# Row statistics for the second layer, taken in a round of attention instead of among the expert units

## The chip, the cores and the metric

The kernel runs on one core of one Trainium2 chip. The metric is the device time of one execution in microseconds (us); lower is better. Five engines of the core work side by side, each through its own queue in program order: TensorE (PE in the profile, with its weight loads as PEld), VectorE (DVE), ScalarE (ACT), GpSimd (POOL) and SyncE (SP), which issues the DMAs. They wait for each other through semaphores. "Busy" shares of different engines overlap.

## The reference, cut to what matters

Two layers work on x of shape (8 batches, 512 rows, 128 columns). In outline:

```
xn = layernorm(x)                                  # per row
x  = x + attention0(xn) + experts(xn)              # 16 heads of 64, causal; 32 experts, top 6, and a shared one
xn = layernorm(x)                                  # per row: mean and variance of the NEW x
x  = x + attention1(xn) + ffn1(xn)                 # attention1 starts with an RMS norm of xn
```

The change concerns the second `layernorm`: for each row of the new x, the mean m and the variance v, then 1/sqrt(v + eps), and beside it the root that the RMS norm of the normalized row needs, 1/sqrt(v/(v + eps) + eps_rms).

## The kernel before

The first layer handles one batch after the other, b = 0 to 7. A batch has two phases.

**Rounds.** Attention of the first layer goes in 8 rounds (`PAIRS`), p = 0 to 7, with two heads in a round. TensorE computes the scores of round p in three chunks (`score0`, the last one, chunk 2, only when the exponentials of chunk 0 are done, L1526), ScalarE takes the exponentials (L731), TensorE turns (transposes) the blocks of probabilities of round p - 1 in five steps (`turn_step`, L1391), VectorE copies four of the turned banks out of PSUM (`take_turned`, L1074) and ScalarE the fifth, and TensorE multiplies them with the values (`weigh_pair`, L1413). So the slot of round p on TensorE holds the turns and the weighing of round p - 1. VectorE also takes the maxima of each row of scores (`row_maxima`, L1083), before which no exponential of the chunk can start.

The order of the steps on each engine is written out by hand. On VectorE a round p > 0 is: copy turned steps 0 and 1 of the round before; maxima of chunk 0; `invert_sums`; `rest_q` (in round 7 `add_rows` instead, which adds the first layer's result of the batch before to x); copy steps 3 and 2; maxima of chunk 2; `rest_k` (not in round 7); maxima of chunk 1; and at the end `route(b, p)`, one piece per round of the choice of experts. In rounds 6 and 7 that piece is the first-layer statistics of the next batch: `stats0` (four `bn_stats`, L972) and `variances0` (L978, L980); for the last batch there is neither.

Two waits tie TensorE to this order. Turn step 4 writes the PSUM bank that step 0 used, so it waits for VectorE's copy of step 0 (`pe.wait_ge(pt_ready, rnd * (TURNS - 1) + 1)`). And chunk 2 of the scores waits for the exponentials of chunk 0, which wait for their maxima.

**Units.** Then 17 expert units, u = 0 to 16 (`units`): TensorE projects a unit (L64 to L66), ScalarE takes a SiLU, VectorE multiplies (`gate` L1112, `hidden` L1122), the result is split in a high and a low part (ScalarE, and VectorE L1116 or GpSimd L541), and TensorE multiplies with the down weights. Between the units stands the preparation of the next batch: rows are normalized after unit 1, and from unit 12 on the next batch's values are projected.

**Statistics for the second layer.** `row_stats(b, ...)` issues on VectorE four `bn_stats` (L1181), a wait for them, four `bn_aggr` (L1184), a wait for them, and two small `tensor_scalar` (L1186, L1187); the last raises `x1_var_ready`. `inv_sqrt1(b)` issues on GpSimd six small operations (L589 to L594), the first and the last of them powers of -0.5; it raises `x1_rstd_ready`. Before the change, batch b - 1's `row_stats` stands in unit 12 of batch b (b = 1 to 6), and its `inv_sqrt1` follows after all of GpSimd's unit work of batch b. The new rows of batch b - 1 are complete in round 7 of batch b (`add_rows`). The first reader of any of these results is `norm_rows1`, in unit 5 of batch 7. Batches 6 and 7 have their statistics taken inside the second layer, which the change leaves alone.

GpSimd has nothing to do in the rounds but `inv_sqrt0(b + 1)` (L508), which waits for `variances0` of round 7; after it come its low parts and divisions of the units.

Of the kernel before, what the change touches and what calls it, by code (L numbers as in the profile page):

```python
# [15 lines left out]
B, T, D = 8, 512, 128  # L16
# [65 lines left out]
def build(nc, a, out_dram):  # L82
    with ExitStack() as ctx:
        def sb(name, shape, dt=F32):
            return ctx.enter_context(nc.sbuf_tensor(name, shape, dt))

        def sem(name):
            return ctx.enter_context(nc.semaphore(name))


        x_all = sb("x_all", [P, B, TILES, D])
# [241 lines left out]
        x1_var_ready = sem("x1_var_ready")  # L333
# [53 lines left out]

        NORM_AFTER, STATS1_AFTER, ROWS_AFTER, LOGITS_AFTER, QK_AFTER, V_AFTER = 1, 12, 5, 7, 9, 12  # L390

        ROWS1_AFTER, TURN1_AFTER = [5, 7, 9], [8, 10, 12]

# [103 lines left out]
        def _(pool):  # L497
# [7 lines left out]
            def inv_sqrt0(b):  # L505
                s = slice(b * TILES, (b + 1) * TILES)
                pool.wait_ge(var_ready, b + 1)
                pool.tensor_tensor(rstd[:, s], var[:, s], mhalf[:, s], ALU.pow).then_inc(rstd_ready, 1)  # L508
# [34 lines left out]
            def units(b):  # L543
                for u in POOL_LO:
                    low_part(b, u)
                    for p in POOL_LO[u]:
                        divide_pair(b, p)

            def split_down(k):
                u = DOWN_PIECES[k]  # L550
                pool.wait_ge(down_hi_ready, k + 1)
                pool.tensor_tensor(down_lo[:, u, :], down_raw[:, u, :], down_hi[:, u, :].bitcast(F32), ALU.subtract).then_inc(down_lo_ready, 1)
# [23 lines left out]
            def second_layer_weights():  # L576
                for part in range(3):
                    bias_part(part)
                setup.step(pool.tensor_copy(wf, qw))
                setup.step(pool.tensor_scalar(wf, wf, 1.0 / 7.5, -1.0, ALU.mult, ALU.add))  # L580
                setup.step(pool.tensor_tensor(wf, wf, qs, ALU.mult))
                pool.wait_ge(lora_taken, 2)
                pool.tensor_tensor(lin[:, :, :], lin[:, :, :], wf, ALU.add).then_inc(lin_ready, 1)

            def inv_sqrt1(b):

                s = slice(b * TILES, (b + 1) * TILES)
                pool.wait_ge(x1_var_ready, b + 1)
                setup.step(pool.tensor_tensor(rstd[:, s], var[:, s], mhalf[:, s], ALU.pow))  # L589
                pool.tensor_tensor(nmr[:, s], nmean[:, s], rstd[:, s], ALU.mult)  # L590
                setup.step(pool.tensor_tensor(rsmall[:, 1, s], rstd[:, s], rstd[:, s], ALU.mult))
                setup.step(pool.tensor_tensor(rsmall[:, 1, s], rsmall[:, 1, s], mv[:, s, 1], ALU.mult))
                setup.step(pool.tensor_scalar(rsmall[:, 1, s], rsmall[:, 1, s], EPS_RMS, None, ALU.add))
                pool.tensor_tensor(rsmall[:, 0, s], rsmall[:, 1, s], mhalf[:, s], ALU.pow).then_inc(x1_rstd_ready, 1)  # L594
# [4 lines left out]
            for k in range(len(DOWN_PIECES)):  # L599
                split_down(k)  # L600
            for b in range(B):
                if b < B - 1:
                    inv_sqrt0(b + 1)
                units(b)
                if b == 0:
                    second_layer_weights()
                elif b < B - 1:
                    inv_sqrt1(b - 1)
            for q in range(GROUPS):
                n0 = q * G  # L610

# [354 lines left out]
        def _(dve):  # L966
# [47 lines left out]
            def route_probabilities(b):  # L1014
                dve.wait_ge(rexp_done, b + 1)
                chain.step(dve.tensor_reduce(sm, rexp[:, :, :], AX, ALU.add))
                chain.step(dve.reciprocal(ri, sm))
                chain.step(dve.tensor_tensor(rl[:, :, :], rexp[:, :, :], over_experts(ri), ALU.mult))
                chain.step(dve.tensor_tensor(chosen, rl[:, :, :], ebias[:, :].unsqueeze(1).to_broadcast([P, TILES, E]), ALU.add))

            def route_top():
                for t in range(TILES):
                    last = dve.max(top8[:, t, :], corr[:, t, 0:E])
                chain.step(last)
                chain.step(dve.memset(top8[:, :, TOPK:8], GONE))

            def route_mark():
                dve.wait_ge(mask_ready, 1)
                for t in range(TILES):
                    last = dve.match_replace(left[:, t, :], top8[:, t, :], corr[:, t, :], TAKEN)  # L1030
                chain.step(last)
# [9 lines left out]
            def route_divide():  # L1041
                chain.step(dve.reciprocal(ri, sm))
                dve.tensor_tensor(comb_et, comb[:, :, :], over_experts(ri), ALU.mult).then_inc(comb_ready, 1)

            def route(b, p):
                if p == 1:
                    route_probabilities(b)
                if p == 2:
                    route_top()
                if p == 3:  # L1050
                    route_mark()
                if p == 4:
                    route_weights(b)
                if p == 5:
                    route_divide()
                if p == 6 and b < B - 1:
                    stats0(b + 1)
                if p == 7 and b < B - 1:
                    variances0(b + 1)
# [69 lines left out]
            def first_layer(b):  # L1129
                for p in range(PAIRS):  # L1130
                    n = b * PAIRS + p
                    if p == 0:
                        row_maxima(n, 0)
                        row_maxima(n, 1)
                        rest_q(n + 1, SCALE0)
                        rest_k(n + 1)
                        row_maxima(n, 2)
                    else:
                        take_turned(n - 1, range(0, 2))
                        row_maxima(n, 0)  # L1140
                        invert_sums(n - 1)
                        if p < PAIRS - 1:
                            rest_q(n + 1, SCALE0)
                        elif b:
                            add_rows(b - 1)
                        take_turned(n - 1, [3, 2])
                        row_maxima(n, 2)
                        if p < PAIRS - 1:
                            rest_k(n + 1)
                        row_maxima(n, 1)  # L1150
                    route(b, p)
                n = b * PAIRS + PAIRS - 1
                take_turned(n, range(0, 2))
                invert_sums(n)
                for u in range(UNITS):
                    if u == 0:
                        take_turned(n, [3, 2])
                    gate(b * UNITS + u, u)
                    if u:
                        hidden(b, u)  # L1160
                    if u and u - 1 not in POOL_LO:
                        low_part(b * UNITS + u - 1, u - 1)
                    if b < B - 1:
                        if u == NORM_AFTER:
                            norm_rows(b + 1, xn)
                    if 0 < b < B - 1 and u == STATS1_AFTER:
                        row_stats(b - 1, x_all[:, b - 1, :, :], x1_var_ready)
                    if b < B - 1:
                        if u == ROWS_AFTER:
                            split_xt(b + 1)  # L1170
                        if u == LOGITS_AFTER:
                            take_logits(b + 1)
                        if u == QK_AFTER:
                            rest_q((b + 1) * PAIRS, SCALE0)
                            rest_k((b + 1) * PAIRS)
                low_part(b * UNITS + UNITS - 1, UNITS - 1)

            def row_stats(b, src, out_sem):
                s = slice(b * TILES, (b + 1) * TILES)
                for t in range(TILES):  # L1180
                    last = dve.bn_stats(stats[:, b * TILES + t, :], src[:, t, :])  # L1181
                chain.step(last)
                for t in range(TILES):
                    last = dve.bn_aggr(mv[:, b * TILES + t, :], stats[:, b * TILES + t, :])  # L1184
                chain.step(last)
                dve.tensor_scalar(nmean[:, s], mv[:, s, 0], -1.0, None, ALU.mult)  # L1186
                dve.tensor_scalar(var[:, s], mv[:, s, 1], EPS, None, ALU.add).then_inc(out_sem, 1)  # L1187
# [8 lines left out]
            for b in range(B):  # L1196
                first_layer(b)
# [9 lines left out]
            for q in range(GROUPS):  # L1207
# [57 lines left out]
                for r in range(2 * G + 1):  # L1265
# [19 lines left out]
                    if q == 0 and r in (3, 5):  # L1285
                        b = B - 2 + r // 4
# [576 lines left out]
```

## Time and profile before

| | |
|---|---|
| median of 3 runs | 1237.54 us (1235.39 to 1241.89) |
| the profiled execution, its own time | 1236.49 us |
| span of the profile, first to last instruction | 1234.7 us |
| PE / DVE / ACT / POOL busy | 97% / 79% / 67% / 33% |
| granted TensorE clock, mean | 0.996 of full speed |

A timeline row gives the start, the duration, the engine, the line, the operation, output<-inputs by the program's names, shapes, and how many in a row were merged ("x2"); in brackets stands the idle time of the engine just before it and what ended it. Names of tiles that share memory are sometimes taken for one another (a hidden activation can be called qk_lo, the third buffer of the gates probs). Ends of matmuls are modelled, so their starts are what can be compared. Times are us from the span's start.

### The profile page before, as it was taken

The page shows a single profiled execution, that of the slowest core. Times are in us where ns is not written, and L with a number is a line of the kernel's source. Part 1 is how long each engine was busy: PE and PEld are TensorE (multiplying, and loading weights), DVE is VectorE, ACT ScalarE, POOL GpSimd, SP SyncE. Part 2 cuts the span into 40 slices and gives each one's busy share as a digit, 9 for nine tenths or more (in the row PEclk, how much of TensorE's full clock was granted, in tenths as well). Part 3 has the DMA queues.
Part 4 walks back from the last instruction along what each step waited for, and adds up shares of the span by engine and source line. Part 5 has one row for each costly group of instructions (what it writes and reads, how often), then busy time and mean ns, then how long its engine had stood idle before and what let it go on. Part 6 is the DMA issues. An engine that isn't in the chain of part 4 may idle for free.

```text
span 1234.7 us, 25147 instructions
## 1 busy us (share of the span) xinstructions
PE 1199.8 (97%) x9508; PEld 903.2 (73%) x9508; DVE 981.3 (79%) x1898; ACT 822.4 (67%) x2173; POOL 412.3 (33%) x371
## 2 busy tenths in 40 slices
PE   6999999999999999999999999999999999998997
PEld 4777777767776777777867786778677767767775
DVE  5888588868896889688968896889687876888785
ACT  6775577557756775677557755775576667676775
POOL 1336420640063006300730072007200859326910
PEclk9999999999999999999999999999999999999999
DMA  7004300410041004100410040015001500000000
GB/s 252 2 19 138 98 1 20 130 60 2 27 128 55 2 29 135 46 2 29 146 36 1 29 150 31 2 30 162 17 2 39 171 1 1 10 11 18 2 10 27
DMA packets 44280, 64.01 MB, mean 52 GB/s; under 512 B 8128, under 2 KB 18368, under 8 KB 43904
## 3 DMA queue, kind: packets, MB, share of 16 engines
q1 hardware_dynamic: 44160, 62.39, 16.0%
q8 instruction: 77, 1.26, 0.4%
q14 instruction: 43, 0.35, 0.1%
HBM read 59.48 MB, written 2.88 MB: 51 GB/s over the span
## 4 chain that ended last, share of the span: by engine, by line
PE 83%; DVE 7%; ACT 4%; POOL 3%; DMA 1%; issue 1%; SPq 1%; POOLq 0%; DVEq 0%
PE psum L1391 14%; PE psum L1363 14%; PE psum L1413 12%; PE psum L64 10%; PE psum L66 10%; PE psum L65 10%; PE psum L1452 4%; PE psum L1368 2%; ACT probs L731 2%; PE psum L1322 1%; PE psum L1417 1%; DVE mneg L1083 1%; DVE stats L1181 1%; PE psum L1618 1%; DMA crow<-weights 1%
## 5 line engine op out<-in xcount | busy, mean ns | idle before, releaser
L731 ACT ACTIVATE probs<-psum,mneg 128x512 f32<-128x512 f32 (+3 forms) x640 | 330.4, 530 | 142.5 <-DVE mneg L1083 138.2
L1083 DVE TENSOR_REDUCE mneg<-psum 128x2 f32<-128x1024 f32 (+2 forms) x320 | 254.2, 820 | 124.6 <-PE psum L1368 121.8
L1391 PE MATMUL psum<-ident,probs 128*128 128x128 f32 x1600 | 225.9, 279 | 9.0 <-ACT pt L752 3.7
L1074 DVE COPY pt<-psum 128x512 f32<-128x512 f32 x320 | 206.1, 683 | 30.0 <-PE psum L1391 27.6
L1391 PEld LDWEIGHTS psum<-ident,probs 128*128 128x128 f32 x1600 | 177.5, 141 | 42.9 <-issue 24.0
L541 POOL TENSOR_TENSOR qk_lo<-sg,qk_hi 128x512 fp32r<-128x512 f32 x64 | 91.9, 1442 | 167.4 <-ACT qk_hi L775 167.4
L508 POOL TENSOR_TENSOR rstd<-var,mhalf 128x4 f32<-128x4 f32 x8 | 8.1, 1018 | 409.4 <-DVE var L980 409.4
L1413 PE MATMUL psum<-pt,v_all 128*64 128x384 f32 (+5 forms) x1088 | 142.6, 412 | 0.0
L731 ACT ACTIVATION_READ_ACCUMULATOR probs<-psum,mneg 128x1 f32 x640 | 131.9, 206 | 0.0
L1363 PE MATMUL psum<-qk_hi 64*128 64x512 f32 (+7 forms) x640 | 122.8, 379 | 1.2 <-ACT probs L731 1.1
L1413 PEld LDWEIGHTS psum<-pt,v_all 128*64 128x64 f32 (+1 forms) x1088 | 69.7, 135 | 63.0 <-issue 50.6
L64 PE MATMUL psum<-xt_hi,gu_hi 128*128 128x512 f32 x272 | 110.8, 408 | 0.4 <-DVE sg L1112 0.4
L65 PE MATMUL psum<-xt_lo,gu_hi 128*128 128x512 f32 x272 | 107.6, 396 | 0.0
L66 PE MATMUL psum<-xt_hi,gu_lo 128*128 128x512 f32 x272 | 107.2, 394 | 0.0
L537 POOL TENSOR_TENSOR yt<-yt,rrow 128x512 f32<-128x512 f32 x64 | 99.5, 1559 | 23.2 <-DMA rrow<-sums 22.9
L1122 DVE TENSOR_TENSOR sg<-sg,crow 128x512 f32<-128x512 f32 x88 | 97.6, 1109 | 7.3 <-DMA crow<-weights 4.4
L1363 PE MATMUL psum<-qk_lo,qk_hi 64*128 64x512 f32 (+7 forms) x640 | 103.2, 318 | 0.0
L1363 PE MATMUL psum<-qk_hi,qk_lo 64*128 64x512 f32 (+7 forms) x640 | 103.0, 317 | 0.0
L785 ACT ACTIVATE sg<-psum 128x512 f32<-128x512 f32 x96 | 57.2, 596 | 58.0 <-PE psum L66 57.9
L1363 PEld LDWEIGHTS psum<-qk_hi 64*128 64x128 f32 (+1 forms) x640 | 60.1, 184 | 45.9 <-issue 44.4
L1112 DVE TENSOR_TENSOR sg<-sg,psum 128x512 f32<-128x512 f32 x96 | 65.3, 680 | 23.3 <-ACT sg L785 23.3
L775 ACT ACTIVATE qk_hi<-sg 128x512 fp32r<-128x512 f32 x96 | 60.3, 628 | 29.1 <-DVE sg L1122 29.1
(255 smaller groups left out, 2460.7 us busy)
## 6 DMA issues: line engine op xcount, KB each, us to landing
crow<-weights SPq DMA_DIRECT2D x256, 128.0 KB, 2.9
rrow<-sums SPq DMA_DIRECT2D x128, 128.0 KB, 3.0
gu_raw<-in_gu SPq DMA_DIRECT2D x1, 2176.0 KB, 11.6
x_all<-in_x SPq DMA_DIRECT2D x8, 256.0 KB, 5.4
out_rows<-x_all SPq DMA_DIRECT2D x8, 256.0 KB, 2.3
down_raw<-in_down SPq DMA_DIRECT2D x1, 1088.0 KB, 13.7
wqkv_raw<-in_wqkv SPq DMA_DIRECT2D x1, 896.0 KB, 6.9
wqkv_raw<-in_wqkv SPq DMA_DIRECT2D x1, 512.0 KB, 5.1
```

Of the source, the lines that this page charges most:

```text
L64: nc.tensor.matmul(out, lh, rh, start=start, stop=False, **kw)
L65: nc.tensor.matmul(out, lh, rl, start=False, stop=False, **kw)
L66: return nc.tensor.matmul(out, ll, rh, start=False, stop=stop, **kw)
L537: pool.tensor_tensor(yt[:, p, :], yt[:, p, :], rrow[:, n % RROWS, :], ALU.mult).then_inc(y_divided, 1)
L541: pool.tensor_tensor(hm_lo[u % 3], sg[u % 3], hm_hi[u % 3].bitcast(F32), ALU.subtract).then_inc(pool_lo_ready, 1)
L731: last = act.activation(probs[:, h * HALF + PROB[t]:h * HALF + PROB[t] + w], bank[score_bank(rnd, c) + h][:, o:o + w], ACT.Exp, bias=mneg[ ...
L1074: dve.tensor_copy(turned_rows(rnd)[:, s % 2, :, 3 - s // 2, :], bank[TURN_BANK[s]].rearrange("p (j q) -> p j q", q=P)).then_inc(pt_ready, 1)
L1083: last = dve.tensor_reduce(mneg_h[:, :, t], psum[:, b:b + 2, o:o + P * (t + 1)], AX, ALU.max, negate=True)
L1122: dve.tensor_tensor(sg[u % 3], sg[u % 3], crow[:, m % CROWS, :], ALU.mult).then_inc(hm_ready, 1)
L1363: mm(bank[score_bank(rnd, c) + h][:, o:o + w], ql[r, 0, qs_], kl[r, 1, ks], start=i == 0 and n == 0, stop=False, **K)
L1391: last = nc.tensor.transpose(bank[TURN_BANK[s]][:, i * P:(i + 1) * P], probs[:, v:v + P], ident[:, :])
L1413: last = mm(Y[c:c + m, first * P:T], v(k), rows_t[:, k, first:TILES, :].rearrange("p t q -> p (t q)"), start=(k == 0), stop=(k == TILES - ...
```

## The change

`row_stats` leaves unit 12 of batch b (for batch b - 1) and is issued in round 6 of batch b, behind `route`, for batch b - 2 (b = 2 to 7). `inv_sqrt1` of that batch is issued on GpSimd ahead of `inv_sqrt0(b + 1)` and of the units of batch b, instead of behind the units. Both still cover batches 0 to 5.

```diff
-        NORM_AFTER, STATS1_AFTER, ROWS_AFTER, LOGITS_AFTER, QK_AFTER, V_AFTER = 1, 12, 5, 7, 9, 12
+        NORM_AFTER, ROWS_AFTER, LOGITS_AFTER, QK_AFTER, V_AFTER = 1, 5, 7, 9, 12
+
+        STATS1_ROUND = 6
@@ GpSimd
             for b in range(B):
+                if b > 1:
+                    inv_sqrt1(b - 2)
                 if b < B - 1:
                     inv_sqrt0(b + 1)
                 units(b)
                 if b == 0:
                     second_layer_weights()
-                elif b < B - 1:
-                    inv_sqrt1(b - 1)
@@ VectorE, rounds of first_layer
                     route(b, p)
+                    if b > 1 and p == STATS1_ROUND:
+                        row_stats(b - 2, x_all[:, b - 2, :, :], x1_var_ready)
@@ VectorE, units of first_layer
-                    if 0 < b < B - 1 and u == STATS1_AFTER:
-                        row_stats(b - 1, x_all[:, b - 1, :, :], x1_var_ready)
```

## Rows read from the trace of the kernel before

**Rows 1.** The page, part 1: busy us (share), instructions of each engine.
```profile
PE 1199.8 (97%) x9508; PEld 903.2 (73%) x9508; DVE 981.3 (79%) x1898; ACT 822.4 (67%) x2173; POOL 412.3 (33%) x371
```

**Rows 2.** Stretch, length, busy PE PEld DVE ACT POOL (instructions), clock, DMA, GB/s.
```profile
281.35:403.24 121.89, 121.89 (x905) 90.87 (x907) 100.24 (x177) 79.53 (x209) 33.37 (x26) 1.00 0.17 54
...
768.76:890.41 121.65, 121.65 (x907) 90.94 (x907) 99.82 (x177) 79.62 (x209) 33.44 (x26) 1.00 0.17 54
...
325.38:333.37 7.99, 7.99 (x87) 6.17 (x89) 7.54 (x15) 5.66 (x19) 0.00 (x0) 1.00 0.01 2
```

**Rows 3.** Waits of TensorE's weight loads, 150 to 955 us: us in total, times, longest.
```profile
PEld psum L64 <- DVE sg L1112: 2.7, 6, 0.8
...
PEld psum L64 <- ACT v_all L740: 1.1, 3, 0.4
```

**Rows 4.** Timeline of VectorE, batch 2, end of round 6 and round 7.
```profile
326.62 1.28 DVE L1083 TENSOR_REDUCE mneg<-psum 128x2 f32<-128x768 f32 x2
327.82 0.86 DVE L972 BATCH_NORM_STATS2 stats<-x_all 128x6 f32<-128x128 f32 x4
328.72 1.29 DVE L1074 COPY pt<-psum 128x512 f32<-128x512 f32 x2
329.92 1.22 DVE L1083 TENSOR_REDUCE mneg<-psum 128x2 f32<-128x1024 f32 x1
...
331.72 1.28 DVE L1074 COPY pt<-psum 128x512 f32<-128x512 f32 x2
333.41 1.56 DVE L1083 TENSOR_REDUCE mneg<-psum 128x2 f32<-128x512 f32 x2 [0.41 <-PE psum L1368]
```

**Rows 5.** Timeline of TensorE, slot 7 of batch 2.
```profile
329.61 0.66 PE L1391 MATMUL psum<-ident,probs 128*128 128x128 f32 x4
...
332.68 0.39 PE L1363 MATMUL psum<-qk_hi 64*128 64x256 f32 x2
...
333.30 2.16 PE L1413 MATMUL psum<-pt,v_all 128*64 128x384 f32 x16
```

**Rows 6.** Timeline of ScalarE, last step of chunk 0's exponentials, round 7 of batch 2.
```profile
332.43 0.20 ACT L731 ACTIVATION_READ_ACCUMULATOR probs<-psum,mneg 128x1 f32 x1
```

**Rows 7.** Timeline of VectorE, units 12 and after, batch 2.
```profile
373.16 0.86 DVE L1181 BATCH_NORM_STATS2 stats<-x_all 128x6 f32<-128x128 f32 x4
...
374.62 0.68 DVE L1112 TENSOR_TENSOR sg<-sg,psum 128x512 f32<-128x512 f32 x1
...
379.74 0.69 DVE L1112 TENSOR_TENSOR sg<-sg,psum 128x512 f32<-128x512 f32 x1 [1.06 <-ACT sg L785]
```

**Rows 8.** Timeline of TensorE, the late start at unit 12, batch 2.
```profile
366.75 0.51 PE L64 MATMUL psum<-xt_hi,gu_hi 128*128 128x512 f32 x1
```

**Rows 9.** Timeline of VectorE, batch 7, end of round 6 and round 7.
```profile
935.69 1.28 DVE L1083 TENSOR_REDUCE mneg<-psum 128x2 f32<-128x768 f32 x2
937.38 1.29 DVE L1074 COPY pt<-psum 128x512 f32<-128x512 f32 x2 [0.41 <-PE psum L1391]
938.79 1.23 DVE L1083 TENSOR_REDUCE mneg<-psum 128x2 f32<-128x1024 f32 x1
```

**Rows 10.** Timeline of TensorE, chunk 2 of the scores, round 7 of batch 7.
```profile
941.73 0.36 PE L1363 MATMUL psum<-qk_hi 64*128 64x256 f32 x2
```

**Rows 11.** Timeline of GpSimd, batch 2: the root in round 7, and inv_sqrt1's first and last.
```profile
335.87 1.01 POOL L508 TENSOR_TENSOR rstd<-var,mhalf 128x4 f32<-128x4 f32 x1 [70.25 <-DVE var L980]
...
382.27 1.45 POOL L589 TENSOR_TENSOR rstd<-var,mhalf 128x4 f32<-128x4 f32 x1
...
386.18 1.03 POOL L594 TENSOR_TENSOR rsmall<-rsmall,mhalf 128x4 f32<-128x4 f32 x1
```

**Rows 12.** Lines L1186, L980, L1094: duration ns min/median/max, first and last start us.
```profile
L1186 DVE TENSOR_SCALAR nmean<-mv x32: 169/170/1204, 252.3 to 1154.1; 128x4 f32<-128x4 f32 x32
L980 DVE TENSOR_SCALAR var<-mv x8: 169/170/171, 4.9 to 823.0; 128x4 f32<-128x4 f32 x8
L1094 DVE RECIPROCAL rinv<-rsum x80: 190/193/205, 31.0 to 1224.7; 128x8 f32<-128x8 f32 x80
```

## The prediction

> **What bounds the kernel now.** I read the page's busy shares first [rows 1]: TensorE 97%, VectorE 79%, ScalarE 67%, GpSimd 33%. That names a suspect, no more. Next the busy time by stretch [rows 2]: from the first weighing of one batch to that of the next (121.9 us in batch 2, 121.65 in batch 6) TensorE's busy time is equal to the length of the stretch, at the full granted clock, and VectorE is busy 100 of 122 us. Then the waits [rows 3]: over the first layer from 150 us on, TensorE's weight loads wait six times for `gate` (2.7 us in all) and three times for a copied value bank (1.1 us); nothing else of weight holds TensorE up. So the first layer is one dense queue of TensorE work. A microsecond that another engine saves gives nothing unless it removes one of those few waits, and a microsecond by which another engine comes late where TensorE has no reserve is added whole.
>
> What matters is therefore the reserve at the two places, old and new, and not VectorE's share.
>
> **The work moved, on VectorE.** In unit 12 of batch 2 the four `bn_stats` begin at 373.16 and the next `gate` at 374.62 [rows 7]: `row_stats` takes 1.46 us of VectorE's time, its two chain waits included. (One of its small operations, L1186, is 0.17 us in the median and 1.20 at most [rows 12], so in some batches it holds VectorE about a microsecond longer in the old place.)
>
> **What the removal gives.** The `gate` of 374.62 comes up to 1.46 us earlier in batches 1 to 6. VectorE catches up by itself: it stands idle 1.06 us before the gate at 379.74, waiting for ScalarE [rows 7]. The late start of TensorE in these units, at 366.75 [rows 8], comes more than six microseconds before the statistics begin at 373.16, so it isn't theirs. I found no late TensorE start between them and the end of the units. I take 0. The bounds: at best all of the waits in [rows 3] go, 2.7 + 1.1 = 3.8 us; at worst nothing.
>
> **What the addition costs, batches 2 to 6.** VectorE in round 6 of batch 2 [rows 4]: the last maxima start at 326.62, `stats0` at 327.82, the copies of turned steps 0 and 1 at 328.72, the maxima of chunk 0 of round 7 at 329.92. No idle time stands between these rows: VectorE arrives there behind TensorE's turns, with nothing to give. `row_stats` goes between 327.82's group and 328.72, and all that follows moves by 1.46 us. Two waits of TensorE hang on it:
> - Turn step 4 starts at 329.61 [rows 5] and needs the copy of step 0. Two copies take 1.29 us from 328.72 [rows 4], so the first ends near 329.37, and the reserve is about 0.24 us. TensorE would stand some 1.2 us here.
> - Chunk 2 of the scores starts at 332.68 [rows 5]. It needs the exponentials of chunk 0, whose last instruction ends at 332.43 + 0.20 = 332.63 [rows 6]: no reserve at all. These exponentials follow maxima that start at 329.92 and move by 1.46. The two delays run beside each other, since the 1.2 us of the first are part of the same lateness: the maxima need a bank that TensorE wrote before turn 4. So by chunk 2 TensorE is 1.46 us late in all.
> - The weighing at 333.30 [rows 5] needs copies that begin at 331.72 and end 1.28 us later, at 333.00 [rows 4]; both sides move by 1.46, so nothing is added.
>
> After that VectorE again waits for TensorE (0.41 us before 333.41 [rows 4]); its backlog is gone, but TensorE's is not, as its queue has no idle time later in which to make it up. The cost is 1.46 us a batch, for the five batches 2 to 6: 7.3 us.
>
> **Batch 7.** It has no `stats0`, so `row_stats` fills some of that room. Its last maxima start at 935.69 [rows 9]; in batch 2 the next group began 327.82 - 326.62 = 1.20 us after that [rows 4], here 936.89. Plus 1.46 gives copies at 938.35, and the maxima of chunk 0 1.21 us later, at 939.56, against 938.79 before [rows 9]. In batch 2 chunk 2 could start 332.68 - 329.92 = 2.76 us after the start of those maxima [rows 4, 5], here 942.32, against 941.73 [rows 10]: 0.6 us. The first layer loses 7.3 + 0.6 = 7.9 us.
>
> **The roots on GpSimd.** They ran behind the units and nobody waited; their removal there gives 0. In the new place they start when `row_stats` ends, near 328.72 + 1.46 = 330.2, and from first start to last end they took 386.18 + 1.03 - 382.27 = 4.94 us [rows 11]: done near 335.1. The root that the next batch waits for starts at 335.87 before and 1.46 later after [rows 11]. They fit in front of it, so it isn't late, and GpSimd has no work in slot 7 (0.00 busy) up to the next weighing [rows 2]. I take 0; the bounds are 0 and a root late by as much as the six operations last, 4.9 us.
>
> One more thing is to be weighed. VectorE's small `tensor_scalar` L1186 is 169 to 1204 ns, while the reciprocal L1094 stays within 190 to 205 over 80 times and L980, which has GpSimd idle beside it, at 169 to 171 [rows 12]. So a form like L1186 can be held up to 1.03 us by a running GpSimd instruction, and a reciprocal has not been. In the new slot the roots run beside VectorE's work of round 7.
> The Trainium skill ("SBUF — State Buffer", Who interferes with whom) has it that VectorE and GpSimd share a port pair that is locked for a whole instruction, and that `tensor_scalar` can take it. The spread of L1186 agrees. By that rule L980 would be the one at risk in the new place, which is the third rival below.
>
> **Second layer.** It starts from batch 7 and moves with it; the first reader of the roots in unit 5 of batch 7 asks for batch 0 to 2, whose roots are done batches before. 0. No DMA is issued or moved; SP's stores of the experts' weights start from TensorE's turn in slot 7 and move along with it.
>
> **The sum.** 1236.49 + 7.9 = 1244.4 on the profiled execution's own time. The median of the runs shown is 1237.54, 1.05 above that execution, and would give 1245.4. I take the middle, 1244.9. What this kernel's measurement can tell from no change is about 0.5%, 6.2 us, so slower begins at 1243.7.
>
> **Rivals.**
> 1. *Not slower: the lateness is absorbed.* Place: the copy of step 0 and the maxima of chunk 0. For it: VectorE has idle time in the slot, 7.99 - 7.54 = 0.45 us by the stretch [rows 2], more in others, and TensorE's ends are modelled, so a reserve may be hidden in its records. Against: 332.63 against 332.68, and L1363 at 332.68 waits in the code. If TensorE had a hidden reserve of 1.46 us in each of these six places, the rounds would cost 0, and the units would give 0 to 3.8 us: 1236.5 down to 1232.7 on the profiled execution, 1233.8 to 1237.5 by the median. It decides at a reserve of 1.46 us; below that the rest is paid. Half of the lateness hidden (0.73) gives about 1240.5.
> 2. *The two waits add up instead of running beside each other*: 1.22 + 1.46 us a batch, because ScalarE's copy of turn 4 stands ahead of the exponentials in its queue. 5 x 2.68 = 13.4, and some 1 us in batch 7: 1251 to 1252. Against: the moved copy by ScalarE would be ready before the moved maxima.
> 3. *GpSimd's roots hold VectorE's L980* by up to 1.03 us in five batches, of which some hides in the idle time behind it: at most 5 x 1.03 = 5.2 more, 1250; I would expect half of it, 1247.5. Against: the roots should be done near 335.1, before L980.
>
> **How the numbers follow.** Forecast 0.74, of it some 0.05 under 1243.7; absorbed wholly or by half 0.17 (wholly, with a gain over 0.5%, 0.03); added waits 0.04; contention 0.05. The forecast's own range is 1243 to 1248. For 8 in 10 the range is 1240.5 to 1249: it takes in half of the lateness absorbed and the likely contention. Faster by over 0.5%: 0.03. Slower: 0.69 + 0.04 + 0.05 = 0.78, less what the two medians can wander: 0.74. Same: 0.23.
>
> **What would show it.** In the changed kernel: copies in round 7 starting 1.4 to 1.5 us later behind `stats0`; an idle time of TensorE before turn step 4 of about 1.2 us released by L1074, and a short one before chunk 2 released by L731; the slot between two weighings 9.45 us in place of 7.99 in batches 2 to 6, 8.6 in batch 7, and unchanged in batch 1, which has no new work there; batches 2 to 6 each 1.46 us longer; the stretch of units as long as before. I am wrong if slot 7 keeps 7.99 (a reserve that I don't see), if the units shorten (a wait of unit 12 that I missed), or if the next batch's rows come late behind GpSimd.

## The result, and the profile after

The changed kernel takes 1248.45 us (median of 4 runs, 1247.31 to 1248.66) against 1237.34 us for the kernel before (4 runs, 1235.39 to 1241.89). The ratio is 1.008, 95% interval 1.006 to 1.010: slower by 7 to 12 us. The forecast was 1244.9 us in a range of 1240.5 to 1249.0. A later measurement of the same kernel, beside 23 runs of the one before, gave 1.0068 (1.0056 to 1.008), which is 8.4 us (6.9 to 9.9).

The page, part 1, of the kernel after, to be held against [rows 1]. All shares are as they were; a share doesn't show this change.
```profile
PE 1203.8 (97%) x9508; PEld 906.1 (73%) x9508; DVE 985.3 (79%) x1898; ACT 822.4 (66%) x2173; POOL 403.4 (32%) x371
```
The stretch shows it. The same slot 7 of batch 2, from the weighing of round 5 to that of round 6 (length, busy PE, PEld, DVE, ACT, POOL, clock): 9.45 us in place of 7.99 [rows 2]. (The row of before lies 0.07 us behind the weighings at both ends; by their starts they stand at 325.31 and 333.30, which gives the same 7.99.) TensorE's busy time is now less than its stretch, by 1.34 us; GpSimd has 2.82 us of roots there.
```profile
328.40:337.85 9.45, 8.11 (x90) 6.20 (x86) 8.94 (x25) 5.66 (x19) 2.82 (x6) 1.00 0.01 2
```
VectorE in that slot, kernel after, answers to [rows 4]. Its lines have moved by two.
```profile
329.71 1.28 DVE L1085 TENSOR_REDUCE mneg<-psum 128x2 f32<-128x768 f32 x2
330.91 0.86 DVE L974 BATCH_NORM_STATS2 stats<-x_all 128x6 f32<-128x128 f32 x4
331.81 0.87 DVE L1183 BATCH_NORM_STATS2 stats<-x_all 128x6 f32<-128x128 f32 x4
332.71 0.38 DVE L1186 BATCH_NORM_AGGREGATE mv<-stats 128x2 f32<-128x6 f32 x4
333.13 0.17 DVE L1188 TENSOR_SCALAR nmean<-mv 128x4 f32<-128x4 f32 x1
333.20 0.17 DVE L1189 TENSOR_SCALAR var<-mv 128x4 f32<-128x4 f32 x1
333.27 1.28 DVE L1076 COPY pt<-psum 128x512 f32<-128x512 f32 x2
334.47 1.22 DVE L1085 TENSOR_REDUCE mneg<-psum 128x2 f32<-128x1024 f32 x1
...
337.96 1.89 DVE L1085 TENSOR_REDUCE mneg<-psum 128x2 f32<-128x512 f32 x3 [0.41 <-PE psum L1370]
```
The copies follow `stats0`'s start by 333.27 - 330.91 = 2.36 us, before by 0.90: 1.46 more. The idle 0.41 us at the end is there as before: VectorE is level with TensorE again, and the lateness is now TensorE's.

TensorE in the same slot answers to [rows 5]: the scores of chunk 0 end, then a wait, turn step 4, chunk 2 (337.23), the weighing.
```profile
332.54 0.23 PE L1370 MATMUL psum<-hide,later 64*128 64x64 bf16 x4
334.11 0.63 PE L1393 MATMUL psum<-ident,probs 128*128 128x128 f32 x4 [1.34 <-DVE pt L1076]
...
337.23 0.39 PE L1365 MATMUL psum<-qk_hi 64*128 64x256 f32 x2
...
337.85 2.16 PE L1415 MATMUL psum<-pt,v_all 128*64 128x384 f32 x16
```
Counted from the weighing that begins the slot (325.31 before, 328.40 after), turn step 4 starts 1.41 us later than before and chunk 2 1.46 us later.

ScalarE's last step of the chunk 0 exponentials, as in [rows 6]: it ends at 337.18, and chunk 2 starts 0.05 us behind it.
```profile
336.98 0.20 ACT L733 ACTIVATION_READ_ACCUMULATOR probs<-psum,mneg 128x1 f32 x1
```
GpSimd's first and last instruction of `inv_sqrt1` and the root that follows, answering to [rows 11]. The six end at 336.60, and the root of the next batch starts 3.8 us later.
```profile
333.45 1.01 POOL L591 TENSOR_TENSOR rstd<-var,mhalf 128x4 f32<-128x4 f32 x1 [69.26 <-DVE var L1189]
...
335.56 1.04 POOL L596 TENSOR_TENSOR rsmall<-rsmall,mhalf 128x4 f32<-128x4 f32 x1
340.41 1.01 POOL L510 TENSOR_TENSOR rstd<-var,mhalf 128x4 f32<-128x4 f32 x1 [3.81 <-DVE var L982]
```
TensorE's waits for VectorE's copies over the first layer from 150 us on (total, times, longest). Before there was none; now there are six, one for each batch with the new work: 1.34 us in batches 2 to 6 and 0.43 in batch 7.
```profile
PE psum L1393 <- DVE pt L1076: 7.1, 6, 1.3
```

**Where the time went.** The spans differ by 1245.5 - 1234.7 = 10.8 us. I split them at the weighings. Slots behind round 6: 9.45, 9.46, 9.44, 9.45, 9.45 in batches 2 to 6 in place of 7.99 each, and 8.54 in place of 7.96 in batch 7: 7.30 + 0.58 = 7.88 us. The rest of the way from the first weighing to the last: 0.47 (in all 924.54 against 916.19). Behind the last weighing: some 0.35 less. Ahead of the first weighing: 2.82 us (36.40 against 33.58), before any instruction that the change touched.

Those 2.82 us are TensorE's rate at the start. Matmuls of 512 columns, kernel before, then kernel after, in the projection of the values: starts 0.24 us apart before, 0.43 us after, where the closer spacing began at 20.97.
```profile
16.57 0.39 PE L65 MATMUL psum<-wqkv_lo,xt_hi 128*128 128x512 f32 x1
16.81 0.40 PE L66 MATMUL psum<-wqkv_hi,xt_lo 128*128 128x512 f32 x1
```
```profile
18.41 0.63 PE L65 MATMUL psum<-wqkv_lo,xt_hi 128*128 128x512 f32 x1
18.84 0.63 PE L66 MATMUL psum<-wqkv_hi,xt_lo 128*128 128x512 f32 x1
...
20.97 0.49 PE L65 MATMUL psum<-wqkv_lo,xt_hi 128*128 128x512 f32 x1
21.30 0.40 PE L66 MATMUL psum<-wqkv_hi,xt_lo 128*128 128x512 f32 x1
```
512 columns at 1.2 GHz are 0.43 us, so up to there TensorE ran at the lower of its two levels, although the clock column of that stretch reads 1.00. The trace's first record of the clock stands at 13.85 us in the kernel before and at 21.16 in the changed one, just where the spacing narrows; the column counts time without a record as 1.00. Whether this belongs to the change is the first question below.

### The profile page after: what moved, and what is told of

Its sections match the earlier page's. It is cut to its first block, busy times and chain, and to the rows that moved or that the text cites. A ratio compares the mean times of both kernels' runs of the same rounds, so it can differ in the third digit from the quotient of the medians.

```text
span 1245.5 us, 25142 instructions
## 1 busy us (share of the span) xinstructions
PE 1203.8 (97%) x9508; PEld 906.1 (73%) x9508; DVE 985.3 (79%) x1898; ACT 822.4 (66%) x2173; POOL 403.4 (32%) x371
## 4 chain that ended last, share of the span: by engine, by line
PE 79%; DVE 10%; ACT 4%; POOL 3%; issue 1%; SPq 1%; DMA 1%; POOLq 0%; DVEq 0%
PE psum L1393 14%; PE psum L1365 14%; PE psum L1415 11%; PE psum L64 10%; PE psum L66 9%; PE psum L65 9%; PE psum L1454 4%; DVE mneg L1085 2%; PE psum L1370 2%; ACT probs L733 2%; PE psum L1324 1%; DVE stats L1183 1%; PE psum L1419 1%; PE psum L1620 1%; DVE probs L1124 1%
## 5 line engine op out<-in xcount | busy, mean ns | idle before, releaser
L1124 DVE TENSOR_TENSOR sg<-sg,crow 128x512 f32<-128x512 f32 x88 | 100.8, 1146 | 5.9 <-DMA crow<-weights 2.9
```

Of the source, the lines that this page charges most:

```text
L1124: dve.tensor_tensor(sg[u % 3], sg[u % 3], crow[:, m % CROWS, :], ALU.mult).then_inc(hm_ready, 1)
```

## Experiments

Each kernel was profiled once and timed beside the kernel before. "Slot 7" is the stretch from the weighing of round 5 to that of round 6 (7.99 before), which the expectations call the slot behind round 6; "weighings" is the way from the first weighing to the last, less the 916.19 us of the kernel before. The stretches of units alone vary by some tenths each from profile to profile, so the sum is good to about 0.9 us and a single slot to 0.02. In batch 0's units alone, where all kernels do the same, eleven of the thirteen profiles took 64.3 to 64.6 us, and only those of the kernel before and of "round0" 63.8: the way in the kernel before is a short one, by some 0.5 us.

| kernel | slot 7, batches 2-6 / 7 | weighings | first weighing at | ratio (95%) |
|---|---|---|---|---|
| changed | 9.45 / 8.54 | +8.4 | 36.40 | 1.008 (1.006-1.010) |
| again | 9.45 / 8.54 | +8.1 | 35.72 | 1.0068 (1.0056-1.008) |
| stats_only | 9.45 / 8.55 | +7.9 | 36.60 | 1.0061 (1.0047-1.0076) |
| roots_only | 7.99 / 7.96 | +0.9 | 36.08 | 1.0019 (1.0008-1.003) |
| round0 | 7.99 / 7.96 | -0.6 | 33.58 | 1.0004 (0.9993-1.0014) |
| half | 8.89 / 7.99 | +5.2 | 33.59 | 1.0042 (1.0026-1.0058) |
| double | 10.36 or 11.85 / 9.46 | +18.1 | 35.32 | 1.0155 (1.0136-1.0174) |
| round5 | 7.99 / 7.95 | +2.0 | 35.60 | 1.0012 (1.0001-1.0023) |
| stats0_early | 8.55 / 8.55 | +3.3 | 36.02 | 1.0023 (1.0007-1.0038) |
| behind_maxima | 9.30 / 9.11 | +8.3 | 36.40 | 1.0046 (1.0028-1.0064) |
| round7 | 7.99 / 7.95 | +4.6 | 35.76 | 1.0026 (1.0013-1.0039) |
| both_round0 | 7.95 / 7.96 | +0.6 | 36.49 | 0.9992 (0.9979-1.0005) |

**again**: the changed kernel, no edit.

> The changed kernel once more. Its profile began its rounds 2.82 us later than the kernel before (first weighing at 36.40 against 33.58), because the first matmuls of 512 columns ran 0.43 us apart up to 21 us instead of 14 us. Theory A: this belongs to the execution, not to the change. Then the first weighing lies anywhere between about 33.5 and 36.5 us, and from there to the end the time is 7.9 us above the kernel before, the slots behind round 6 being 9.45 us (batches 2 to 6), 8.54 (batch 7) and 7.99 (batches 0... 1). Theory B: the change makes the start later. Then the first weighing is at 36.4 again and all executions stand about 11 us above the kernel before, with no spread beyond 0.5 us.

The six executions spread over 4.7 us (1242.55 to 1247.29), the profiled one began its weighings at 35.72, not at 36.40, and the slots came out to the hundredth. Over all kernels the first weighing lay between 33.58 and 36.60: the kernels "round0" and "half", which touch as little of the start as the others, had the early one. The same kernel began at two different times, and its executions spread by far more than the 0.5 us that theory B allows, so theory B is out as it was put. That the whole 2.8 us go with the execution is argued from "round0" and "half"; the changed kernel itself was never profiled with the early start. The 11.1 us by which the first runs stood above the kernel before were to some part such starts; how large a part can't be said, as the other timed executions have no trace. The overlap of the two intervals (7.4 to 9.9) holds the 7.9.

**stats_only**: only VectorE's part.
```diff
             for b in range(B):
-                if b > 1:
-                    inv_sqrt1(b - 2)
                 if b < B - 1:
                     inv_sqrt0(b + 1)
                 units(b)
                 if b == 0:
                     second_layer_weights()
+                elif b > 1:
+                    inv_sqrt1(b - 2)
```


> Only the statistics move to round 6; the roots of batch b - 2 stay behind the units of batch b on GpSimd. Theory A (VectorE's 1.46 us in front of the copies is the whole cost): slots of 9.45 us in batches 2 to 6 and 8.5 in batch 7, as in the changed kernel, and 7.9 us above the kernel before from the first weighing on. Rival (the roots beside round 7 hold VectorE up): slots shorter than 9.45 by as much as the roots cost, up to 1.0 us, and 2.9 to 7.9 us in all.

Slots of 9.45 and 8.55: all of the cost is there without the roots. The contention rival is out.

**roots_only**: the kernel before, with `inv_sqrt1(b - 2)` ahead of the units of batch b for b > 1, in place of `inv_sqrt1(b - 1)` behind them.

> Only the roots move: batch b - 2's roots stand ahead of the units of batch b, the statistics stay in unit 12. Theory A: no change, slots of 7.99 us, within 0.3 us of the kernel before from the first weighing on. Rival (roots cost something): over 0.5 us more.

The slots are unchanged. The weighings are 0.9 us longer, in the stretches of units; over half of it is batch 0's (64.33 against 63.81), where the two kernels do the same. The time is 1.0019, 1 to 4 us over the kernel before, which the slots don't explain; in the profile it sits in a late first weighing and in the second layer (287.5 against 284.9 us behind the last weighing). The granted clock goes with the latter. Behind the last weighing, its fall at the very end of the program left out, TensorE spent 13.7 us at the lower of its two levels in "roots_only" and "round7" (287.5 and 287.0 us), 6.8 in the kernel before and the changed one (284.9 and 284.6), and 3.4 in "double" and "behind_maxima" (283.0 and 283.7). What set this number in each execution stays open, and with it whether the roots have a part in the 1 to 4 us; what they have none in is the 7.9 us.

**round0**: the statistics at the front of round 0.
```diff
                     if p == 0:
+                        if b > 1:
+                            row_stats(b - 2, x_all[:, b - 2, :, :], x1_var_ready)
                         row_maxima(n, 0)
@@
                     route(b, p)
-                    if b > 1 and p == STATS1_ROUND:
-                        row_stats(b - 2, x_all[:, b - 2, :, :], x1_var_ready)
```


> The statistics of batch b - 2 stand at the very front of round 0 of batch b, ahead of the first maxima, where VectorE was idle for 3.75 us in batch 3; the roots as in the changed kernel. Theory A (only the reserve at the place counts): 1.46 us fit in 3.75, so all slots are 7.99 us and the time is that of the kernel before within 0.3 us. Rival (VectorE's work costs in any round, 1.46 us a batch): 7 to 9 us more than before.

No cost, with the same instructions and the same roots ahead of the units. VectorE at the start of batch 2's rounds in this kernel: the statistics run, and 2.29 us of idle time are still left.
```profile
263.88 0.87 DVE L1181 BATCH_NORM_STATS2 stats<-x_all 128x6 f32<-128x128 f32 x4
264.78 0.38 DVE L1184 BATCH_NORM_AGGREGATE mv<-stats 128x2 f32<-128x6 f32 x4
265.19 0.17 DVE L1186 TENSOR_SCALAR nmean<-mv 128x4 f32<-128x4 f32 x1
265.27 0.16 DVE L1187 TENSOR_SCALAR var<-mv 128x4 f32<-128x4 f32 x1
267.72 1.23 DVE L1083 TENSOR_REDUCE mneg<-psum 128x2 f32<-128x1024 f32 x1 [2.29 <-PE psum L1368]
```

**half**: in round 6 only the four `bn_stats` and their wait; the rest of `row_stats` in unit 12 of the same batch, the roots behind the units.

> Only the four bn_stats and their wait (0.90 us of VectorE) stand in round 6; bn_aggr, mean and variance stand in unit 12 of the same batch, the roots behind the units. Theory A (no reserve, slope 1): slots of 7.99 + 0.90 = 8.89 us in batches 2 to 6, some 8.0 in batch 7 (its 0.41 us of idle time and 0.19 us of earlier maxima take up most of it), 4.5 us in all. Rival (there is a reserve of some tenths and then a steeper price): under 8.7 us.

8.89 and 7.99 us: the price is 0.90 us for 0.90 us of VectorE, so the first tenths are paid like the rest. There is no hidden reserve, and batch 7's 0.41 us of idle time takes up what it was expected to.

**double**: the four `bn_stats` and their wait twice in round 6.

> The changed kernel with the four bn_stats and their wait issued twice (same values): 2.36 us of VectorE in round 6. Theory A: the two waits of TensorE run beside each other, slope 1: slots of 7.99 + 2.36 = 10.35 us in batches 2 to 6, 9.4 in batch 7, 13.3 us above the kernel before. Rival (the waits at turn 4 and at chunk 2 add up once the lateness is large): over 10.8 us a slot.

Two answers. In batches 2 and 5 the slot is 10.36 us, as theory A says, and 9.46 in batch 7: the waits don't add up. In batches 3, 4 and 6 it is 11.85, 11.83 and 11.85, over the 10.8 that was to speak for the rival; but the rival's second wait isn't there. In all six slots TensorE has one idle time, ahead of turn step 4 (2.25 us, 1.34 in batch 7), and none ahead of chunk 2. Batch 3's slot shows what is longer: the four transposes of L1463 take 1.06 us in place of 0.60, the eight of L1396 1.91 in place of 1.04.
```profile
458.09 0.63 PE L1396 MATMUL psum<-ident,probs 128*128 128x128 f32 x4 [2.25 <-DVE pt L1076]
458.56 0.36 PE L1489 MATMUL psum<-ident,rexp 128*128 128x128 f32 x1
458.71 1.06 PE L1463 MATMUL psum<-ident,rrow 128*128 128x128 f32 x4
459.57 1.91 PE L1396 MATMUL psum<-ident,probs 128*128 128x128 f32 x8
```
The busy time by stretch in the same place has the reason in its clock column (third from the right). The 0.60 and the 0.87 are means over stretches that hold both levels; from 459 to 462 us the clock is 0.50, the lower one.
```profile
455.50:458.00 2.50, 0.35 (x8) 0.11 (x4) 2.40 (x14) 0.82 (x6) 0.56 (x1) 1.00 0.00 0
458.00:461.00 3.00, 2.91 (x16) 2.94 (x17) 2.81 (x5) 1.89 (x5) 2.26 (x6) 0.60 0.00 0
461.00:465.00 4.00, 4.00 (x45) 2.79 (x45) 2.60 (x5) 1.16 (x7) 0.00 (x0) 0.87 0.21 53
459.00:462.00 3.00, 3.00 (x16) 2.67 (x16) 2.65 (x5) 1.97 (x6) 1.42 (x3) 0.50 0.00 0
```
Batches 4 and 6 have such a stretch behind the same idle time, batches 2 and 5 have none.

**round5**: `STATS1_ROUND = 5`.

> The same statistics at the end of round 5. There VectorE is idle for 0.82 us before the maxima of the next round, turn step 4 comes 1.3 us after its copy, and chunk 2 0.38 us after its exponentials. Theory A: turn 4 has reserve but for 0.16 us, the maxima come 1.46 - 0.82 = 0.64 late, chunk 2 about 0.3 us late: slots of round 6 9.1 us in place of 8.81 in batches 2 to 7, slots of round 7 unchanged at 7.99, 1.9 us in all. Rival (1.46 us of VectorE cost 1.46 in any dense round): 8.8 us in all.

The slot ahead of it, that of round 6, is 9.01 us in place of 8.81 in each of batches 2 to 7: 0.20 us a batch, and nothing behind it. The size is near the 0.3 expected, the place isn't: TensorE waits at turn step 4, and chunk 2 has a reserve then.
```profile
324.18 0.63 PE L1393 MATMUL psum<-ident,probs 128*128 128x128 f32 x4 [0.15 <-DVE pt L1076]
```
The same 1.46 us of VectorE cost a seventh one round earlier.

**stats0_early**: the changed kernel with `stats0(b + 1)` at the front of round 0 instead of in round 6.

> The changed kernel with the first layer's bn_stats of the next batch taken at the front of round 0 instead of in round 6, so that each of batches 2 to 6 looks like batch 7. Theory A: slots of 8.54 us in batches 2 to 7, 3.4 us above the kernel before; batches 0 and 1 unchanged. Rival (the place behind round 6 costs 1.46 whatever stands ahead of it): slots of 9.45.

8.55 us in every batch. Taking the 0.90 us of `stats0` out from ahead gives back 0.90 us: the two sets of statistics compete for one reserve.

**behind_maxima**: the statistics in round 7, between `row_maxima(n, 0)` and `invert_sums(n - 1)`.

> The same statistics one step later on VectorE: in round 7 behind the maxima of chunk 0, ahead of the reciprocal, so that turn step 4 and chunk 2 of the scores are on time and only the copies of steps 3 and 2 are late. Theory A (the price is the lateness less the reserve of the next wait): the weighing had 0.24 us of reserve, so slots of 7.99 + 1.22 = 9.21 us in batches 2 to 6 and 9.0 in batch 7, 7.2 us in all. Rival (the cost of the change comes from the maxima and the exponentials alone): slots of 7.99 to 8.3.

9.30 and 9.11 us, 0.1 more than expected. The wait has moved to the weighing, as it should.
```profile
338.03 2.16 PE L1415 MATMUL psum<-pt,v_all 128*64 128x384 f32 x16 [1.24 <-DVE pt L1076]
```

**round7**: `STATS1_ROUND = 7`.

> The same statistics at the end of round 7, behind the variances of the next batch. VectorE was idle there for 0.51 us before its next copies, and turn step 4 started 0.2 us after its copy. Theory A: the copies come about 0.86 us late, so the slot after this (7.44 us) becomes 8.1 in batches 2 to 6 and 7.5 in batch 7, where there are no variances; slots behind round 6 stay at 7.99; 3.4 us in all. Rival (1.46 us a batch whatever the place): slots of 8.9, 8.8 us in all.

The stretch behind slot 7 is 8.22 us in batches 2 to 6 (7.44 before; 8.1 expected) and 7.75 in batch 7 (7.5 expected): 4.2 us in all, where 3.4 were expected. TensorE waits at turn step 4 of the turns of round 7:
```profile
340.28 0.63 PE L1393 MATMUL psum<-ident,probs 128*128 128x128 f32 x4 [0.59 <-DVE pt L1076]
```

**both_round0**: "round0" with `stats0(b + 1)` at the front of round 0 too.

> Both kinds of statistics (batch b - 2's for the second layer, batch b + 1's for the first) at the front of round 0, 2.36 us into an idle time of 3.75 us; none in round 6. Theory A: no cost there, and chunk 2 of the scores in round 7 no longer waits the last hundredths: slots of 7.96 us in place of 7.99, at best 0.2 us below the kernel before, which is not to be told from no change. Rival (round 6 without any statistics is worth something): slots below 7.9.

Slots of 7.95 to 7.96 and a ratio of 0.9992 (0.9979 to 1.0005): the 0.03 us a batch are there, and they can't be told from no change. No kernel here beats the one before by a measurable amount.

## Why the prediction was right

- *TensorE's queue bounds the first layer, so only the reserve at the new place counts.* Shown: the same instructions cost 0 in round 0, 0.20 us a batch in round 5, 1.46 behind round 6, 1.31 one step later, 0.78 behind round 7.
- *1.46 us of VectorE ahead of the copies, paid in full in batches 2 to 6: 7.3 us.* Measured 7.30. "half" and the clean slots of "double" give slope 1 on both sides of it.
- *Two waits, beside each other.* Shown in the trace after: 1.34 us of idle time at turn step 4 (I said some 1.2). It starts 1.41 us late and chunk 2, 0.05 us behind its exponentials, 1.46: of the second wait hardly anything is left. "double", where only the first shows, rules out that they add up.
- *Batch 7: 0.6 us.* Measured 0.58; "stats0_early" shows by putting every batch in that state that it is the missing `stats0` that does it.
- *The removal gives nothing.* "round0" removes it too and gains nothing that shows: 1.0004. (L1186 held VectorE about a microsecond longer in the old place in one batch only, 1.20 us at 860.32 while a GpSimd instruction ran; in the other five it took at most 0.42.)
- *The roots cost nothing.* Right for the slots ("stats_only"). They are even shorter than the 4.94 us that I took from [rows 11]: 3.15 us from first start to last end (336.60 - 333.45). The place goes with it: in the nine profiles in which they run in the rounds, the six took 3.14 to 3.17 us, and in the four in which they run beside or right behind the units' work (before, "roots_only", "stats_only", "half") 3.6 to 4.96. VectorE's large two-input work in SBUF is in the units, not in the rounds, which I take for the reason; that isn't shown. The contention rival looked at L982, which stayed at 0.17 us; the reciprocal at 335.60 took its usual 0.20 us beside a running root.
- *The sum.* The mechanism gave 7.9 us and the slots measured 7.88. The time missed by more: 1248.45 lies above the forecast's own range of 1243 to 1248. What the 1244.9 lacks is not in the steps: 2.8 us of the profiled execution are its late start. The prediction took the time ahead of the first round as fixed. That the time lies inside 1240.5 to 1249.0 is luck in part, since this range was wide for other reasons (half of the lateness absorbed, contention).

What failed is small: two reserves were put too large. The prediction let turn step 4 start as soon as its copy ends and gave it 0.24 us of reserve. A TensorE instruction that stands waiting starts about 0.15 us behind the end of the copy (334.11 against 333.95, which is 333.27 and the 0.68 us of a 128x512 copy), and the reserve was 0.05: 1.46 less the 1.41 by which turn step 4 is late. It cost the sum nothing, because chunk 2 had none at all. The expectations of "behind_maxima" and "round7" allowed 0.06 us for this start; the missing 0.1 is what "behind_maxima" and batches 2 to 6 of "round7" have over their expectations. Batch 7 of "round7" is 0.25 us over: there the copies also came later than I had reckoned, 0.38 us later behind the weighing than before.

## What to carry to other kernels

Price a moved instruction by the reserve at its new place: follow its engine to the next result that the bounding engine waits for, and subtract the idle time on the way and the time by which that result is early; what is left is paid whole, once for each time round. An engine's mean share (79% here, and unchanged) says nothing of it, and one step of the schedule can be the difference between a seventh of the price and all of it. Look for the long idle time of the helper engine (3.75 us at the front of round 0) and put such work there.

## What the runs showed of the hardware

- TensorE's rate at the start of the program isn't the same from execution to execution. It went from the lower level to the upper at 13.8 to 13.9 us in three of thirteen profiles and between 18.3 and 21.2 in the others (by the first record of the clock and by the narrower spacing of the matmuls), and the first weighing moved with it by up to 3.0 us. Two profiles of one and the same kernel have 18.5 and 21.2. The profile's clock column reads 1.00 through all of this. A difference of 3 us between two single executions of this kernel means nothing before their first weighings have been compared.
- An idle time of TensorE of 2.25 us inside the dense part was followed in three of five cases by a stretch at the lower level (granted clock 0.50 from 459 to 462 us in batch 3), at 1.49 us apiece; idle times of up to 1.34 us there were not, in any kernel here. A stall can so cost more than its length.
- A TensorE instruction that stood waiting for a VectorE copy started 0.15 us behind the copy's end, in every such wait of these kernels.
- The same six small GpSimd operations took 3.15 us in the rounds and 3.6 to 4.96 beside or right behind the units' work.
